# Self-attention cores: probabilities turned four heads at a time, query blocks outermost

## The chip, the core and the metric

The program runs on one NeuronCore of a Trainium2 chip. The engines are TensorE (PE; its weight loads are shown apart as PEld), VectorE (DVE), ScalarE (ACT), GpSimd (POOL) and SyncE (SP), which here only issues DMAs. The metric is the device time of one execution in microseconds, lower is better. The median of three executions of the kernel before is 3642.35 us (3640.83 to 3653.55).

## The reference

A decoder of two layers, each with causal self-attention, cross-attention and a mixture of experts, on x of 2 x 512 tokens of width 512. The change is in the two self-attentions (16 heads of 32). Cut to what matters:

```python
q, k, v = proj(Wq), proj(Wk), proj(Wv)            # B=2, H=16, S=512, dh=32
q, k = _apply_rope(q, cos, sin), _apply_rope(k, cos, sin)   # first layer only
scores = jnp.einsum('bhqd,bhkd->bhqk', q, k) / math.sqrt(dh)
scores = jnp.where(causal, scores, jnp.finfo(jnp.float32).min)
probs = jax.nn.softmax(scores, axis=-1)
attn = jnp.einsum('bhqk,bhkd->bhqd', probs, v)
```

## The kernel before

The stages run one after the other with a barrier between them. `self_attention` (stage names sa0 and sa1; the profile shows both as sa) has four: a layer norm that also turns x (L155, transposes of 128x128), `project_self`, `attention_core` and the output projection (L196). `attention_core` also serves the first cross-attention, where it isn't causal.

Q and K come out of the projection with channels on partitions, four heads of 32 to a chunk of 128, eight chunks (`NI`) for the two sequences. The core splits each value into a high part (L497 on ACT) and the rest (L539 on POOL), and DMAs of 32 rows lay three combinations of the two under each other, so that one product over 96 rows gives nearly exact scores (`packed`, L373 on SP for Q, L550 on POOL for K).

It works on pairs of heads, 16 pairs (`NP`) a core. The scores are made twice. First with queries on the output's partitions (L425, and L427 adds the mask), two heads and one block of 128 queries at a time, for the row maxima (L575 on DVE). The maxima are turned (L438), split into two rows (L503, L584) and laid under `packed` by DMA (L380). Then the scores are made again with keys on partitions, less the maximum (L449 over 98 rows, mask L452). Their exponentials (L511 on ACT) need no turning: they are the moving operand of P times V (L461), whose stationary operand is V beside a block of ones, 64 columns for a head, so that the row sums come out as well. Two heads take columns 0 to 63 and 64 to 127. The result is copied (L517), laid out by four DMAs a pair (L391, L392), and DVE inverts the sums over 128x512 (L590) and multiplies (L592).

Each product of two f32 operands shows as two MATMUL records; a transpose and a product of packed operands (fp32r) show as one.

The order on each engine is written out: TensorE goes through pair j's four key blocks, and behind each comes the P times V of the block before and one query block of pair j+2's maxima. TensorE may start a pair's second scores once `put_rows` has landed, and the maxima of a query block once the block before is reduced.

## Time and profile before

| | |
|---|---|
| median of three executions | 3642.35 us |
| the profiled execution | 3634.11 us, its span 3632.3 us |
| core of sa0, from its barrier to the first product of the output projection | about 123 to 365 us |
| core of sa1 | about 1377 to 1605 us |
| busy over the span | PE 3145.2, DVE 1263.3, ACT 967.4, POOL 975.8 us |
| mean granted TensorE clock | 0.879 |

The profile has one row for each group of instructions with its count and mean, and a trace with the start of each. A granted clock of 0.50 is 1.2 GHz, of 1.00 is 2.4 GHz. A PE record's length holds the way through the array, so what an instruction costs in a stream is the distance from its start to the next one's.

### The profile page before, as it was taken

How to read it: one execution, taken by the hardware profiler on the slowest of the kernel's cores; microseconds unless marked ns; L12 is line 12 of the kernel's file. 1: busy time of each engine (PE TensorE's matmuls, PEld its weight loads, DVE VectorE, ACT ScalarE, POOL GpSimd, SP SyncE). 2: the span in 40 equal slices, each digit the busy share in tenths (PEclk: the TensorE clock that was granted, in tenths of full speed). 3: DMA queues.
4: the chain of work that ended last, by engine and by line, in shares of the span. 5: the costliest groups of instructions: out<-in, count | busy, mean ns of one | idle time of the engine just before them, and what ended most of it. 6: DMA issues, size and time to landing. Idle time of an engine off the chain costs nothing. (4 is left out here: it accounts for less than half of the span.)

```text
span 3632.3 us, 40681 instructions
## 1 busy us (share of the span) xinstructions
PE 3145.2 (87%) x13166; PEld 1910.4 (53%) x13166; DVE 1263.3 (35%) x1863; ACT 967.4 (27%) x2096; POOL 975.8 (27%) x1107
## 2 busy tenths in 40 slices
PE   7898897988559787988996989999999856999997
PEld 3444343333548543447885874555554442777773
DVE  3234335654411213425434225555552131111114
ACT  1233133444101013314332004444442000222220
POOL 2331003220021203303442105555553014222115
PEclk9656897999679887669998999999999957999998
DMA  2232203331059613314443433222220001999996
GB/s 78 56 75 58 84 12 84 75 70 31 25 202 323 222 58 81 80 27 152 142 144 107 142 105 118 68 68 69 71 72 21 25 18 33 340 346 347 331 325 191
DMA packets 317562, 442.93 MB, mean 122 GB/s; under 512 B 45502, under 2 KB 179622, under 8 KB 317448
## 3 DMA queue, kind: packets, MB, share of 16 engines
q1 hardware_dynamic: 276232, 344.96, 29.9%
q0 software_dynamic: 26240, 69.27, 7.0%
q10 hardware_dynamic: 14976, 27.27, 2.1%
q8 instruction: 61, 1.00, 0.1%
q14 instruction: 53, 0.43, 0.0%
HBM read 308.78 MB, written 75.58 MB: 106 GB/s over the span
## 5 line engine op out<-in xcount | busy, mean ns | idle before, releaser
L1379 PE MATMUL ps<-moe_blocks_xgt,moe_blocks_w 128*128 128x128 f32 (+1 forms) x3072 | 364.3, 277 | 7.2 <-DMA moe_blocks_b1s<-rb_cols 4.7
L511 ACT ACTIVATE normed<-ps 128x512 f32<-128x512 f32 (+3 forms) x512 | 247.6, 516 | 427.9 <-PE ps L452 265.2
L1379 PEld LDWEIGHTS ps<-moe_blocks_xgt,moe_blocks_w 128*128 128x128 f32 (+1 forms) x3072 | 350.7, 184 | 13.1 <-issue 12.8
L2258 POOL TENSOR_TENSOR normed<-normed,xa_core_rinv 128x257 f32<-128x257 f32 (+1 forms) x256 | 266.1, 1062 | 273.0 <-DVE xa_core_rinv L2189 273.0
L1361 PE MATMUL ps<-moe_blocks_w,moe_blocks_ht 128*128 128x512 f32 (+1 forms) x624 | 285.1, 593 | 0.0
L2225 ACT ACTIVATE normed<-ps,xa_core_nmax 128x257 f32<-128x257 f32 (+1 forms) x256 | 173.8, 685 | 323.2 <-DVE xa_core_nmax L2184 322.8
L2135 PE MATMUL ps<-xa_core_k,xa_core_q 128*128 128x512 f32 x512 | 242.6, 597 | 14.8 <-DVE xa_core_k L2174 10.9
L2184 DVE TENSOR_REDUCE xa_core_nmax<-ps 128x1 f32<-128x257 f32 (+1 forms) x256 | 164.4, 683 | 250.2 <-PE ps L2135 250.2
L1450 DVE COPY moe_blocks_y<-ps 128x512 f32<-128x512 f32 x104 | 71.9, 692 | 457.4 <-PE ps L1361 457.4
L2161 PE MATMUL ps<-xa_core_pt,xa_core_v 128*128 128x512 f32 x512 | 225.1, 592 | 0.7 <-DVE xa_core_pt L2197 0.7
L578 DVE TENSOR_REDUCE xa_core_nmax<-ps 128x1 f32<-128x1024 f32 x128 | 155.9, 1224 | 133.6 <-PE ps L432 133.6
L575 DVE TENSOR_REDUCE sa_core_nmax<-ps 128x2 f32<-128x256 f32 (+3 forms) x128 | 105.6, 825 | 251.8 <-PE ps L427 251.7
L2149 PEld LDWEIGHTS ps<-identity,normed 128*128 128x128 f32 x1024 | 118.1, 140 | 104.5 <-issue 67.9
L2149 PE MATMUL ps<-identity,normed 128*128 128x128 f32 x1024 | 146.4, 276 | 22.4 <-ACT xa_core_pt L2235 21.5
L1361 PEld LDWEIGHTS ps<-moe_blocks_w,moe_blocks_ht 128*128 128x128 f32 (+1 forms) x624 | 111.1, 191 | 100.5 <-issue 100.5
L1914 POOL TENSOR_TENSOR normed<-normed 128x512 f32<-128x512 f32 x96 | 126.3, 1317 | 138.3 <-DVE normed L1874 138.3
L425 PE MATMUL ps<-sa_core_packed 96*128 96x128 f32 (+3 forms) x256 | 131.0, 571 | 33.3 <-DMA sa_core_packed<-sa_core_parts 23.7
L2161 PEld LDWEIGHTS ps<-xa_core_pt,xa_core_v 128*128 128x128 f32 x512 | 94.8, 190 | 108.1 <-issue 107.1
L461 PE MATMUL ps<-normed,sa_v 128*64 128x256 f32 (+3 forms) x512 | 149.7, 680 | 0.0
L1327 POOL COPY moe_blocks_idx<-moe_index 128x1 uint32 (+1 forms) x104 | 19.2, 185 | 483.1 <-PE ps L1352 438.2
L1400 ACT ACTIVATE moe_blocks_xgt<-ps 128x512 f32<-128x512 f32 x104 | 62.1, 597 | 316.7 <-PE ps L1352 316.7
L461 PE MATMUL ps<-normed,xa_v 128*64 128x512 f32 x512 | 144.1, 643 | 0.0
(292 smaller groups left out, 5447.1 us busy)
## 6 DMA issues: line engine op xcount, KB each, us to landing
moe_blocks_w<-L_ffn_rw SPq DMA_DIRECT2D x80, 704.0 KB
moe_blocks_w<-L_ffn_rw SPq DMA_DIRECT2D x80, 512.0 KB
moe_blocks_w<-L_ffn_w SPq DMA_DIRECT2D x24, 1408.0 KB
moe_y<-moe_blocks_y ACTq DMA_DIRECT2D x104, 256.0 KB
k_raw<-xa_kq_raw SPq DMA_DIRECT2D x64, 256.0 KB, 2.0
v_rows<-normed SPq DMA_DIRECT2D x64, 256.0 KB
xa_core_k<-k_raw SPq DMA_DIRECT2D x32, 512.0 KB, 4.7
xa_core_v<-v_rows SPq DMA_DIRECT2D x32, 512.0 KB
```

The costliest lines, as they stand in the source:

```text
L425: nc.tensor.matmul(g.ps[:, bank + h, 0:w], packed[0:KR, s, h, 0, n * P:(n + 1) * P], packed[0:KR, s, h, 1, 0:w], start=True, stop=False)
L461: nc.tensor.matmul(g.ps[2 * h * DH:2 * (h + 1) * DH, 6 + j % 2, a:S], v[:, j // (H // 2), kb, j % (H // 2), h:h + 2, :].rearrange("p a d - ...
L511: nc.scalar.activation(probs[:, e % RING, a:S], g.ps[:, 4 + h, a:S], ACT.Exp).then_inc(exp_done, 1)
L578: nc.vector.tensor_reduce(nmax[:, j % 2, n:n + 1], g.ps[:, bank:bank + 2, :].rearrange("p a n -> p (a n)"), X_AXIS, ALU.max, negate=True). ...
L1361: mm = nc.tensor.matmul(g.ps[:, 6 + s % 2, :], ht[0:fn, s % 2, f, :], w2s[s][0:fn, f, :], start=(f == 0), stop=(f == NF - 1))
L1379: mm = nc.tensor.matmul(g.ps[0:fn, 2 + s % 2 + 2 * half, f * P:(f + 1) * P], w1s[s][:, k, half * F + f0:half * F + f0 + fn], xgt[:, s % 2, ...
L2135: mm = nc.tensor.matmul(s_ps(n)[:, c:c + 512], q[:, s, qb * P:(qb + 1) * P], k[:, s, c:c + 512], start=True, stop=True)
L2149: mm = nc.tensor.transpose(g.ps[:, 4 + half, m * P:(m + 1) * P], prob[:, nn % PR, c:c + P], g.ident[:, :])
L2161: mm = nc.tensor.matmul(g.ps[:, 6 + hs, :], v[:, hs, m, :], pt[:, hs, m, :], start=(m == 0), stop=(m == NKT - 1))
L2184: ins = nc.vector.tensor_reduce(nmax[:, n % PR, m:m + 1], s_ps(n)[:, lo:hi], X_AXIS, ALU.max, negate=True)
L2225: ins = nc.scalar.activation(prob[:, n % PR, lo:hi], s_ps(n)[:, lo:hi], ACT.Exp, bias=nmax[:, n % PR, m:m + 1], accum_out=rsum[:, n % PR, ...
L2258: ins = nc.gpsimd.tensor_tensor(prob[:, n % PR, lo:hi], prob[:, n % PR, lo:hi], rinv[:, n % PR, m:m + 1].to_broadcast([P, hi - lo]), ALU.mult)
```

## The change

`attention_core` stays for the first cross-attention. The self-attentions get `self_core`:

- Scores are made once, with queries on partitions. A unit is one pair of heads and one block of 128 queries, with the keys up to that block; a chunk of four heads has 8 units (query block outermost, then the two pairs), a core 64.
- DVE reduces the maxima, ACT takes the exponentials with the maximum as bias and the sum accumulated, DVE inverts two numbers a row, POOL multiplies the probabilities by them, TensorE turns them in 128x128 blocks, and DVE (3 of 4 heads) and ACT (1 of 4) copy them to SBUF.
- P times V takes V (32 columns a head) as the stationary operand. Four heads write partitions 0, 32, 64 and 96 of one bank, for one query block of a chunk, one key block after the other.
- Gone are the second scores, the turning, splitting and laying of the maxima, the ones beside V, the layout DMAs and the inversion over 128x512. ACT copies a chunk's result straight to its place.
- The splitting of the first two chunks into parts, and the DMAs that pack them, move into the projection stage. Of later chunks they run in the core, the rest now on DVE, all DMAs on SP (12 a chunk, each with Q and K together).

```diff
+    def low(self, nc, dve, i):
+        dve.wait_ge(self.high_done, i + 1)
+        nc.vector.tensor_tensor(self.parts[i % 2][:, 1:4:2, :], self.qk[:, :, i, :], self.parts[i % 2][:, 0:3:2, :],
+                                ALU.subtract).then_inc(self.low_done, 1)
...
+                if t in (1, 2):
+                    if rope:
+                        act.wait_ge(rotated, len(units))
+                    else:
+                        act.wait_ge(copied, len(units))
+                    heads.high(nc, t - 1)
...
+    NI, QB, U = B * KC, S // P, 2 * (S // P)
+    N = NI * U
+    SKEW, LAG, PR = 3, 2, 6
+    SCORE, TURN, VALUE = (0, 2), (4, 5, 6), 7
...
+                if u >= 2:
+                    pe.wait_ge(exp_done, 2 * (u - 1))
+                t = heads.packed[i % 2]
+                for h in range(2):
+                    nc.tensor.matmul(g.ps[:, bank + h, 0:n], t[:, 2 * p + h, 0, qb * P:n], t[:, 2 * p + h, 1, 0:n],
+                                     start=True, stop=False)
...
+                    for j in range(qb + 1):
+                        mm = nc.tensor.transpose(g.ps[:, bank, j * P:(j + 1) * P],
+                                                 prob[:, 2 * (u % PR) + h, j * P:(j + 1) * P], g.ident[:, :])
...
+                for j in range(qb + 1):
+                    for h in range(HPC):
+                        mm = nc.tensor.matmul(g.ps[h * DH:(h + 1) * DH, VALUE, qb * P:(qb + 1) * P],
+                                              v[:, b, j, c * P + h * DH:c * P + (h + 1) * DH],
+                                              pt[:, at + h, j * P:(j + 1) * P], start=(j == 0), stop=(j == qb))
+                mm.then_inc(pv_done, 1)
...
+            for u in range(N + SKEW):
+                if u < N:
+                    score(u)
+                if u >= SKEW:
+                    turn(u - SKEW)
+                    if u - SKEW >= LAG + 1 and (u - SKEW) % 2 == 1:
+                        i, qb, p, n = place(u - SKEW - LAG)
+                        values(i, qb)
```

TensorE before, in the middle of sa0's core: one key block of a pair, the P times V of the block before it, and one query block of the maxima. L425 and L427 are the maxima's scores, L449 and L452 the second ones, L461 is P times V.

```order
L425 MATMUL ps<-sa_core_packed 128x512
L427 MATMUL ps<-sa_core_mask,identity 128x128
L425 MATMUL ps<-sa_core_packed 128x512
L427 MATMUL ps<-sa_core_mask,identity 128x128
L449 MATMUL ps<-sa_core_packed 128x512
L452 MATMUL ps<-identity,sa_core_mask 128x128
L449 MATMUL ps<-sa_core_packed 128x512
L452 MATMUL ps<-identity,sa_core_mask 128x128
L438 MATMUL ps<-identity,sa_core_nmax 8x128
L461 MATMUL ps<-normed,sa_v 64x128 x2
```

TensorE of the change, at the same place: L390 and L393 are a unit's scores and mask, L412 the transposes of the unit three before (`SKEW`), L429 is P times V of one query block of four heads.

```order
L390 MATMUL ps<-sa_packed 128x256 x2
L393 MATMUL ps<-sa_core_mask,identity 128x128 x2
L412 MATMUL ps<-identity,sa_w 128x128 x8
L429 MATMUL ps<-normed,sa_v 32x128 x12
L390 MATMUL ps<-sa_packed 128x256 x2
L393 MATMUL ps<-sa_core_mask,identity 128x128 x2
L412 MATMUL ps<-identity,sa_w 128x128 x2
L390 MATMUL ps<-sa_packed 128x384 x2
L393 MATMUL ps<-sa_core_mask,identity 128x128 x2
L412 MATMUL ps<-identity,sa_w 128x128 x2
L429 MATMUL ps<-normed,sa_v 32x128 x16
```

The second scores are gone, transposes stand in their place, and P times V comes once in two units, in up to 16 short products instead of two long ones for each key block.

DVE of the change, in the first chunk of a core: L453 is a unit's maxima, L457 the inverted sums of the unit before, L466 and L468 the copies of turned probabilities (two heads, one head), L227 the rest for the chunk after next.

```order
L453 TENSOR_REDUCE sa_core_nmax<-ps 128x2
L457 RECIPROCAL sa_core_rinv<-sa_core_rsum 128x2
L466 COPY normed<-ps 128x2x128
L453 TENSOR_REDUCE sa_core_nmax<-ps 128x2
L457 RECIPROCAL sa_core_rinv<-sa_core_rsum 128x2
L468 COPY normed<-ps 128x128
L227 TENSOR_TENSOR sa_parts<-sa_qk,sa_parts 128x2x512
L453 TENSOR_REDUCE sa_core_nmax<-ps 128x2
L457 RECIPROCAL sa_core_rinv<-sa_core_rsum 128x2
L466 COPY normed<-ps 128x2x256
```

Before, DVE had only the maxima, the small L584 and once in two pairs L590 with L592 between them; now it stands in the path of every unit three times.

## Rows read from the trace of the kernel before

**Rows 1.** Busy time and clock by stretch: both cores, slow and fast stretches, others
```profile
core 0: us, PE busy (x) PEld busy (x) DVE busy (x) ACT busy (x) POOL busy (x), PEclk, DMA share, GB/s
123.00:365.00 242.00, 210.70 (x784) 108.70 (x784) 89.23 (x98) 75.13 (x177) 69.09 (x113) 0.57 0.30 71
1377.00:1605.00 228.00, 194.02 (x784) 100.71 (x784) 89.42 (x98) 74.38 (x177) 68.97 (x113) 0.63 0.32 75
1490.00:1590.00 100.00, 100.00 (x342) 50.15 (x342) 37.98 (x40) 32.26 (x77) 18.97 (x33) 0.50 0.25 59
1406.00:1430.00 24.00, 21.96 (x135) 11.99 (x131) 9.85 (x13) 11.21 (x29) 11.69 (x18) 1.00 0.37 87
2400.00:2700.00 300.00, 288.53 (x1050) 152.68 (x1049) 168.51 (x296) 134.84 (x344) 156.52 (x148) 1.00 0.21 70
1286.00:1290.00 4.00, 4.00 (x21) 4.00 (x20) 2.73 (x6) 2.40 (x4) 0.00 (x0) 0.50 0.79 291
1290.00:1291.50 1.50, 1.48 (x13) 1.25 (x11) 0.00 (x0) 1.34 (x3) 0.00 (x0) 0.97 0.00 0
```

**Rows 2.** The same view of L461 alone; a pair has 16 of its records
```profile
1406.00:1430.00 24.00, 8.16 (x44) 1.98 (x40) 1.00 0.37 87
1490.00:1590.00 100.00, 38.10 (x116) 8.61 (x116) 0.50 0.25 59
```

**Rows 3.** Timeline of PE at 1.2 GHz: start us, length us, then the instruction
```profile
201.72 0.46 PE L449 MATMUL ps<-sa_core_packed 98*128 98x128 f32 x1
...
202.07 0.46 PE L449 MATMUL ps<-sa_core_packed 98*128 98x128 f32 x1
...
202.59 1.12 PE L461 MATMUL ps<-normed,sa_v 128*64 128x256 f32 x4
203.64 0.79 PE L425 MATMUL ps<-sa_core_packed 96*128 96x512 f32 x1
...
204.32 0.77 PE L425 MATMUL ps<-sa_core_packed 96*128 96x512 f32 x1
...
206.85 0.70 PE L461 MATMUL ps<-normed,sa_v 128*64 128x128 f32 x4
207.48 0.47 PE L425 MATMUL ps<-sa_core_packed 96*128 96x128 f32 x1
```

**Rows 4.** Timeline of PE at 2.4 GHz, the same core
```profile
214.46 0.65 PE L461 MATMUL ps<-normed,sa_v 128*64 128x256 f32 x4
215.04 0.50 PE L425 MATMUL ps<-sa_core_packed 96*128 96x512 f32 x1
...
215.43 0.47 PE L425 MATMUL ps<-sa_core_packed 96*128 96x512 f32 x1
...
217.50 0.44 PE L461 MATMUL ps<-normed,sa_v 128*64 128x128 f32 x4
217.87 0.33 PE L425 MATMUL ps<-sa_core_packed 96*128 96x128 f32 x1
...
218.07 0.30 PE L425 MATMUL ps<-sa_core_packed 96*128 96x128 f32 x1
```

**Rows 5.** Timeline of PE in the second cross-attention: transposes of probabilities at 2.4 GHz
```profile
2401.03 1.04 PE L2149 MATMUL ps<-identity,normed 128*128 128x128 f32 x8
```

**Rows 6.** Groups by shape, 2400 to 2700 us: count | busy us, mean ns | idle before
```profile
L2161 PE MATMUL ps<-xa_core_pt,xa_core_v 128*128 128x512 f32 x259 | 114.0, 592 | 0.0
L2258 POOL TENSOR_TENSOR normed<-normed,xa_core_rinv 128x767 f32<-128x767 f32 x66 | 100.0, 1515 | 0.0
...
L2197 DVE COPY xa_core_pt<-ps 128x512 f32<-128x512 f32 x65 | 43.5, 669 | 0.0
L2258 POOL TENSOR_TENSOR normed<-normed,xa_core_rinv 128x257 f32<-128x257 f32 x66 | 40.5, 613 | 142.9 <-DVE xa_core_rinv L2189 142.9
...
L2225 ACT ACTIVATION_READ_ACCUMULATOR normed<-ps,xa_core_nmax 128x1 f32 x131 | 25.7, 196 | 0.0
```

**Rows 7.** The page's costliest groups: maxima of the self-attention cores
```profile
L575 DVE TENSOR_REDUCE sa_core_nmax<-ps 128x2 f32<-128x256 f32 (+3 forms) x128 | 105.6, 825 | 251.8 <-PE ps L427 251.7
```

**Rows 8.** Groups by shape, 156 to 286 us: DVE, ACT
```profile
L511 ACT ACTIVATE normed<-ps 128x512 f32<-128x512 f32 x18 | 10.7, 598 | 25.8 <-PE ps L452 25.2
```

**Rows 9.** Timeline: first product of sa0's core, last values, first product of the projection behind
```profile
134.40 0.45 PE L425 MATMUL ps<-sa_core_packed 96*128 96x128 f32 x1 [12.19 <-DMA sa_core_packed<-sa_core_parts]
...
363.41 0.69 DVE L592 TENSOR_TENSOR sa_qt<-sa_qt,sa_core_total 128x512 f32<-128x512 f32 x1
...
365.32 2.90 PE L196 MATMUL ps<-sa_wo,sa_qt 128*128 128x512 f32 x3 [9.95 <-PEq L67]
```

More of the change, by code:

```diff
@@ L172, in self_attention @@
         w_loaded = [st.sem(f"w_loaded{n}") for n in range(3)]
+        heads = HeadPacks(st, qk)
         def load_weights(sp):
@@ L181, in self_attention @@
         with Stage(nc, name + "_proj") as pr:
-            project_self(nc, g, pr, w, w_loaded, rope, qt, kt, v, wos, wo, wo_loaded, masks, mask)
+            project_self(nc, g, pr, w, w_loaded, rope, qk, v, wos, wo, wo_loaded, masks, mask, heads)
         with Stage(nc, name + "_core") as co:
-            attention_core(nc, g, co, qt, kt, v, ot, S // P, masks)
+            self_core(nc, g, co, heads, v, ot, masks, w)
         with Stage(nc, name + "_out") as ou:
@@ L205, in _, with __init__, high, pack @@
                                                 ALU.add).then_inc(added, 1)
-def project_self(nc, g, st, w, w_loaded, rope, qt, kt, v, wos, wo, wo_loaded, masks, mask):
+class HeadPacks:
+    TERMS = ((0, 0), (1, 0), (0, 1))
+    ROWS = len(TERMS) * DH
+    DMAS = HPC * len(TERMS)
+    def __init__(self, st, qk):
+        self.qk = qk
+        self.parts = [st.sbuf(f"parts{n}", [P, 4, S], F32R) for n in range(2)]
+        self.packed = [st.sbuf(f"packed{n}", [self.ROWS, HPC, 2, S], F32R) for n in range(2)]
+        self.high_done, self.low_done = st.sem("high_done"), st.sem("low_done")
+        self.packed_in = [st.sem(f"packed_in{n}") for n in range(2)]
+    def high(self, nc, i):
+        nc.scalar.activation(self.parts[i % 2][:, 0:3:2, :], self.qk[:, :, i, :], ACT.Copy).then_inc(self.high_done, 1)
+    def low(self, nc, dve, i):
+        dve.wait_ge(self.high_done, i + 1)
+        nc.vector.tensor_tensor(self.parts[i % 2][:, 1:4:2, :], self.qk[:, :, i, :], self.parts[i % 2][:, 0:3:2, :],
+                                ALU.subtract).then_inc(self.low_done, 1)
+    def pack(self, sp, i):
+        sp.wait_ge(self.low_done, i + 1)
+        for h in range(HPC):
+            for r, (qp, kp) in enumerate(self.TERMS):
+                sp.dma_start(self.packed[i % 2][r * DH:(r + 1) * DH, h, :, :].bitcast(F32),
+                             self.parts[i % 2][h * DH:(h + 1) * DH, qp:3 + kp:2 + kp - qp, :].bitcast(F32)
+                             ).then_inc(self.packed_in[i % 2], 16)
+    def wait_packed(self, eng, i):
+        eng.wait_ge(self.packed_in[i % 2], 16 * self.DMAS * (i // 2 + 1))
+def project_self(nc, g, st, w, w_loaded, rope, qk, v, wos, wo, wo_loaded, masks, mask, heads):
     made, copied = st.sem("made"), st.sem("copied")
     v_made, v_copied = st.sem("v_made"), st.sem("v_copied")
-    units = [(c, b, dst, part) for part, dst in enumerate((qt, kt)) for c in range(KC) for b in range(B)]
+    units = [(c, b, qk[:, part, :, :], part) for part in range(2) for c in range(KC) for b in range(B)]
     RAW = 3
@@ L228, in _ @@
             sp.dma_start(masks[:, :], mask).then_inc(wo_loaded, 16)
+            heads.pack(sp, 0)
+            heads.pack(sp, 1)
             sp.wait_ge(wo_loaded, 32)
@@ L276, in _ @@
                 act.wait_ge(v_made, t + 1)
[L277 to L284 removed]
+                nc.scalar.activation(v[:, b, kb, :], g.ps[:, 6 + t % 2, :], ACT.Copy).then_inc(v_copied, 1)
+                if t in (1, 2):
[4 more added lines that the diff above has]
+                    heads.high(nc, t - 1)
+        if rope:
+            @block.gpsimd
+            def _(pool):
                 pool.wait_ge(r_loaded, 48)
@@ L291, in _ @@
                                             ALU.mult).then_inc(cos_done, 1)
[L293 to L304 removed]
+        @block.vector
@@ new lines, in _ @@
+        def _(dve):
+            for j, (c, b, dst, part) in enumerate(units if rope else ()):
+                if j == 0:
+                    dve.wait_ge(r_loaded, 48)
+                dve.wait_ge(swapped, j + 1)
+                nc.vector.tensor_tensor(rs[:, j % 2, :], g.ps[:, 4 + j % 2, :], sin[:, :],
+                                        ALU.mult).then_inc(sin_done, 1)
+                dve.wait_ge(sin_done, j + 1)
+                dve.wait_ge(cos_done, j + 1)
+                nc.vector.tensor_tensor(dst[:, b * KC + c, :], rc[:, j % 2, :], rs[:, j % 2, :],
+                                        ALU.add).then_inc(rotated, 1)
+            heads.low(nc, dve, 0)
+            heads.low(nc, dve, 1)
```

154 lines of the change are left out of this document (130 added, 24 removed).

## The prediction

> **What bounds the kernel now.** First the two stages. The self-attention cores take 242 and 228 us of the span [rows 1], together 470; nothing else in the program is edited but the projections ahead of them. Then who works there. In 1490 to 1590 us TensorE is busy for all of 100.00 us, DVE for 37.98, ACT for 32.26, POOL for 18.97 [rows 1]. So TensorE is the bound. Then its clock: the mean granted clock of the cores is 0.57 and 0.63, and it is 0.50 (1.2 GHz) for the whole of 1490 to 1590, while it is 1.00 in 1406 to 1430 [rows 1]. Then the pace. A pair of heads has 16 records of P times V: 116 in 100 us is 13.8 us a pair at 1.2 GHz, 44 in 24 us is 8.7 us a pair at 2.4 GHz [rows 2]. I count in chunks of four heads: 27.6 us slow, 17.5 us fast, eight chunks a core.
>
> **Does that follow from the parts?** Score products of two heads with their mask: at 128 keys 2 x 0.35 = 0.70 us and at 512 keys 2 x 0.68 = 1.36 us slow [rows 3], 0.40 and 0.78 fast (218.07 less 217.87, 215.43 less 215.04) [rows 4]. The four lengths lie evenly, so a set is 4 x the mean of the ends: 4.1 us slow, 2.4 us fast. P times V of two heads: over 128 queries 0.63 us slow, 0.37 fast; over 256, 1.05 and 0.58 [rows 3, 4]. So 128 queries more cost 0.42 slow and 0.21 fast, on a start of 0.21 and 0.16; the four key blocks (512 to 128 queries) make 5.0 and 2.7 us. A pair is two sets and one P times V: 13.2 slow against 13.8 measured, 7.5 fast against 8.7. Slow, TensorE's own work explains the pace within 5%. Fast, about 16% is waiting on others.
>
> **What goes.** The second scores: 2 x 4.1 = 8.2 us a chunk slow, 4.8 fast. The turned maxima and their DMAs, L590 and the layout DMAs: they were late only at 2.4 GHz and at the ends of the core.
>
> **What TensorE gets.** Transposes: a unit turns 2 blocks for each key block, a chunk 2 x 2 x (1+2+3+4) = 40. The second cross-attention turns the same f32 blocks fast, eight in 1.04 us with the way through the array, so 0.11 to 0.13 each [rows 5]; slow, a layer norm shows 20 weight loads in 4.00 us, 0.20 to 0.21 each [rows 1]. That is 4.6 us fast, 8.4 slow. P times V: 10 key blocks a chunk, each with four heads of 32 columns over 128 queries, 8 records. What this costs no row shows. L461 shows two column groups at work at once: four records of 512 columns one after the other take 0.43 us each in the second cross-attention (114.0 us is 259 records in 300 us, at 592 ns with their way through) [rows 6], 0.11 for 128 columns, while two heads' four records cost 0.21 for 128 and not 0.43. If four groups go at once, a block costs 0.21 fast and 0.42 slow; if only two at once, with the start paid each time, 0.74 and 1.26. I take 0.40 and 0.60, near the lower end: pairs of groups do overlap, but eight short weight loads have little to hide under. A chunk: 4.0 fast (2.1 to 7.4), 6.0 slow (4.2 to 12.6). TensorE's sum for a chunk is then 4.8 + 4.6 + 4.0 = 13.4 us fast and 8.2 + 8.4 + 6.0 = 22.6 us slow.
>
> On how the columns are shared, the Trainium skill (TensorEngine Tiling (Array Packing), Key Properties) says that changing the tiling mode drains the array. The change alternates between full and 32-column products, but so does the kernel before with 64 columns, and the 0.16 to 0.21 us start in my sum is what such a turn shows; charged for every key block instead of every batch it would give about the 0.40 that I take.
>
> **What the others get, a chunk.** DVE: 16 maxima of one head each, in 8 instructions at a mean of 0.825 us [rows 7] = 6.6; copies of 2 and 1 heads over 128 to 512 keys, by 0.669 us for 512 [rows 6] and about 1.05 ns an element more or less: 3.2 + 1.9; the rest of a split over 1024 elements, about 1.2, where L592 is 0.69 for 512 [rows 9]; eight small inversions 1.2. Sum 14.1. ACT: 16 exponentials, where 512 keys take 0.598 [rows 8], 0.44 in the mean, and half of a 0.196 us accumulator read each [rows 6]: 8.6; a quarter of the copies 1.75, high parts 1.05, result 0.6: 12.0. POOL: 0.613 us for 257 and 1.515 for 767 elements [rows 6], so 1.77 ns an element: 0.6, 1.1, 1.5, 2.0 for a unit's 256 to 1024, 10.3 a chunk. SP: 12 DMAs, which have a whole chunk to land. All are under TensorE's slow 22.6; at 2.4 GHz DVE's 14.1 passes TensorE's 13.4 and becomes the bound.
>
> **What ends last at 2.4 GHz.** DVE and TensorE hand over to each other in each unit: reduction waits for scores, scores for the exponentials of two units before, transposes for POOL and for a free bank, the DVE copy for the transposes. Queued behind the copy's wait is the next reduction, for which ACT waits. P times V comes once in two units in one piece (up to 1.6 us), and there DVE waits. The kernel before lost 16% to its waits at that clock; the same on 14.1 gives 16.4. I take 16.5 us a chunk fast; slow 22.6 and 8% for the same reasons, 24.5.
>
> **Head and tail.** The first score of sa0 starts at 134.40, after 12.19 us of waiting for the packing DMAs [rows 9]; the change packs two chunks under the projection of V, which leaves about 1 us. The two high parts and the two rests there lie beside TensorE's products of V, for whose result ACT only has one copy of 512 elements a tile (0.6 us, [rows 8]) and DVE nothing, so they cost nothing; uncovered they would be 2 x (1.05 + 1.2), some 5 us. At the end the last pair's result is laid and inverted until 364.1 and the projection starts at 365.32, 9.95 us after the last product [rows 9]; a copy and a barrier, 2 us, remain. Filling and draining the new chain (POOL 2.0, transposes, copy, last P times V) I put at 8 us. A core is 11 us + 8 chunks.
>
> **The clock.** This decides more than any count. Before, it stayed at 1.2 GHz through 100 us of a full TensorE, and a core in the same shape as the new one, with the same transposes, POOL multiplication and copies, shows 1.00 over 300 us with PE busy for 288.53 [rows 1]. What went ahead of a rise: in the layer norm nothing but transposes, 0.50 until 1290 and 0.97 behind it [rows 1]. The new core replaces half the short packed products by such transposes, and has no DMA or long inversion that stops TensorE for microseconds once it is fast. So I expect 2.4 GHz most of the time, with some 10 us a core lost to slow stretches (two chunks at 24.5 for 16.5 are 16, one is 8).
>
> The Trainium skill (TensorE: Matmul & The Clock Gate, Part 4: PE-mode transpose) says otherwise: a transpose does not count as a busy PE and does not bring the full clock. By it the change would stay slow, which is my first rival. This trace disagrees where it can: the clock rises in a run of f32 transposes alone, from 0.50 to 0.97 [rows 1].
>
> **Forecast.** 11 + 8 x 16.5 = 143, and 10 for slow stretches: 153 us a core, 306 for 470, so 164 less. From the profiled 3634 that is 3470; the median of the runs stands 8 us above it, so 3478.
>
> **Rivals.** 1. The clock stays at 1.2 GHz throughout: 11 + 8 x 24.5 = 207 a core, 56 us less, 3586. For it: 100 us without a rise, and scores of the same kind stay in the mix. 2. The clock changes to and fro, or four column groups don't go at once and a key block costs 0.74 fast: TensorE's 16.8 passes DVE, 19.5 with the handing over; both give a chunk of 19.5 to 20.5, a core of 170 to 180, so 3525 to 3535 (110 to 120 less). 3. Slower than before: the clock stays low and the four heads go two at a time, starting anew each time. A chunk is 8.2 + 8.4 + 12.6 = 29.2 us, a core 245, 20 us more in all: 3662. It decides from 28 us a chunk on, that is from 1.14 us a key block slow; one head at a time (8 x 0.21 and starts) would give 3730. Against it speaks the overlap that L461 already shows. 4. The change doesn't reach its pipelining: DVE's order makes each unit wait for the one before, 20 us a chunk; this falls on the time of rival 2.
>
> **How the numbers follow.** Forecast 0.50, rival 1 0.17, rivals 2 and 4 together 0.24, rival 3 0.05, better than all of them (15 us a chunk and no slow stretch, 3450 and below) 0.04. The range 3440 to 3592 takes in the forecast with a chunk of 15 to 18, rival 2 and rival 1. A measurement of this kernel tells 0.5%, 18 us: faster 0.92, the same 0.04, slower 0.04.
>
> **What would show it.** In the profile of the changed kernel: granted clock near 1.00 in both cores, cores of 150 us; transposes 0.11 us apart; a key block's eight records within 0.40 us; DVE busy 110 us a core and PE's longest waits on DVE or POOL; first scores within 2 us of the barrier, the output projection 2 us behind the last P times V. A clock of 0.50 with PE full is rival 1, and eight records over 0.7 us rival 2. The forecast is wrong if the clock stays low, or if POOL's multiplication over two heads takes much more than 2 us.

## The result and the profile after

| | before | after |
|---|---|---|
| median of the runs, us | 3643.27 (3640.83 to 3653.55, 4 runs) | 3456.27 (3445.77 to 3463.13, 4 runs) |
| ratio to before | 1 | 0.9479 (95% interval 0.9444 to 0.9514) |
| span of the profiled run, us | 3632.3 | 3444.0 |
| mean granted clock of the span | 0.879 | 0.920 |
| core of sa0 / sa1, us | 242 / 228 | 136.9 / 139.5 |

The change takes 187 us off the median and 188 off the span. The two cores lose 470.2 less 276.4 = 194 us, a little more than that, so all of the gain is there. Here and below a core's length runs from DVE's cast of the mask, the first instruction behind the barrier, to the first product of the output projection.

The lines of the changed kernel that the rows name: L390 score products, L393 the mask's product, L412 transposes, L429 P times V, L453 maxima, L457 inversions, L466 and L468 DVE's copies of turned probabilities, L498 ACT's, L487 exponentials, L510 POOL's multiplication, L223 high and L227 rest of a split, L476 the copy of a result, L196 the projection behind.

Busy time and clock by stretch, the view of [rows 1]: both cores; one chunk in the middle; the slow stretch near the start of sa0's core, and the 75 us behind it:

```profile
core 0: us, PE busy (x) PEld busy (x) DVE busy (x) ACT busy (x) POOL busy (x), PEclk, DMA share, GB/s
123.50:260.40 136.90, 112.33 (x1217) 77.56 (x1217) 101.38 (x199) 92.21 (x303) 79.60 (x64) 0.94 0.32 71
1274.50:1414.00 139.50, 115.64 (x1216) 80.24 (x1217) 101.64 (x199) 92.18 (x303) 79.61 (x64) 0.90 0.32 69
163.30:179.60 16.30, 13.24 (x154) 9.10 (x153) 12.84 (x26) 11.53 (x39) 9.94 (x9) 1.00 0.50 110
...
128.00:138.00 10.00, 8.47 (x38) 5.31 (x39) 7.64 (x14) 6.77 (x23) 5.29 (x5) 0.50 0.00 0
...
143.00:218.00 75.00, 60.38 (x705) 41.18 (x705) 59.78 (x117) 52.89 (x173) 44.22 (x38) 1.00 0.45 98
```

The granted clock went from 0.57 and 0.63 [rows 1] to 0.94 and 0.90. TensorE is busy for 82% of sa0's core and DVE for 74%: no engine is full.

Timeline of PE in sa0's core, the view of [rows 3, 4]: start us, length us, instruction, and in brackets the idle time ahead of it and who ended it:

```profile
123.82 0.44 PE L390 MATMUL ps<-sa_packed 96*128 96x128 f32 x2 [1.93 <-DVE sa_core_mask L447]
...
172.82 0.65 PE L429 MATMUL ps<-normed,sa_v 128*32 128x128 f32 x16
173.40 0.44 PE L390 MATMUL ps<-sa_packed 96*128 96x128 f32 x2
...
173.80 1.04 PE L412 MATMUL ps<-identity,sa_w 128*128 128x128 f32 x8
174.60 0.48 PE L390 MATMUL ps<-sa_packed 96*128 96x256 f32 x2
...
176.74 0.86 PE L429 MATMUL ps<-normed,sa_v 128*32 128x128 f32 x24
...
179.60 1.08 PE L429 MATMUL ps<-normed,sa_v 128*32 128x128 f32 x32
...
185.19 0.43 PE L429 MATMUL ps<-normed,sa_v 128*32 128x128 f32 x8 [0.74 <-ACT sa_qk L476]
...
257.01 1.93 PE L429 MATMUL ps<-normed,sa_v 128*32 128x128 f32 x56
260.39 1.96 PE L196 MATMUL ps<-sa_wo,sa_qk 128*128 128x512 f32 x4 [1.45 <-PEq L67]
```

The four query blocks of a chunk have 1 to 4 key blocks of eight records each. They take 0.43, 0.65, 0.86 and 1.08 us with the way through the array. From the start of a batch to the start of the next product it is 0.36, 0.58, 0.79 and 1.01 us (173.40 less 172.82 is 0.58): 0.14 us and 0.22 for each key block. Batches of 32 records start at 146.98, 163.30, 179.60, 195.90 and 212.21 us, so a chunk is 16.3 us. Eight transposes take 1.04 us, as in [rows 5], and 0.80 from start to the next start, 0.10 each.

The waits of the changed kernel, 139 to 250 us: engine and line, who is waited for, us in total, times, longest:

```profile
POOL sa_w L510 <- DVE sa_core_rinv L457: 43.9, 42, 2.1
ACT sa_w L487 <- DVE sa_core_nmax L453: 34.0, 37, 1.7
DVE sa_core_nmax L453 <- PE ps L393: 18.1, 22, 1.8
PEld ps L412 <- DVE normed L466: 14.8, 28, 0.8
...
PEld ps L412 <- ACT normed L498: 8.4, 19, 0.9
PE ps L412 <- DVE normed L466: 7.6, 20, 0.6
...
PE ps L429 <- ACT sa_qk L476: 5.2, 7, 0.7
```

It is a ring: DVE waits for scores, ACT for DVE's maxima, POOL for DVE's inversions, and TensorE for the two copies that free its banks. One more wait, of P times V for ACT's copy of the last chunk's result, comes once a chunk. In the chunk of 16.30 us above, the timeline of DVE shows 3.45 us of idle time: 2.29 waiting for scores, 0.52 for the high part, 0.38 for transposes and 0.26 for an exponential.

Groups by shape, 139 to 258 us, the view of [rows 6] (count, busy us, mean ns, idle before); they are DVE's maxima and copies, the rest of a split, and POOL's longest:

```profile
L510 POOL TENSOR_TENSOR sa_w<-sa_w,sa_core_rinv 128x1024 f32<-128x1024 f32 x16 | 30.0, 1893 | 10.0 <-DVE sa_core_rinv L457 10.0
...
L453 DVE TENSOR_REDUCE sa_core_nmax<-ps 128x2 f32<-128x1024 f32 x14 | 17.0, 1216 | 7.6 <-PE ps L393 7.6
...
L466 DVE COPY normed<-ps 128x1024 f32<-128x1024 f32 x8 | 9.8, 1224 | 3.8 <-PE ps L412 3.8
...
L227 DVE TENSOR_TENSOR sa_parts<-sa_qk,sa_parts 128x1024 fp32r<-128x1024 f32 x5 | 7.5, 1495 | 2.6 <-ACT sa_parts L223 2.6
```

### The profile page after: what moved, and what is told of

Read it like the earlier page. It is cut to its first block and busy times, and to the rows that moved or that the text cites. A ratio compares the mean times of both kernels' runs of the same rounds, so it can differ in the third digit from the quotient of the medians.

```text
span 3444.0 us, 42500 instructions
## 1 busy us (share of the span) xinstructions
PE 2962.6 (86%) x14027; PEld 1856.9 (54%) x14030; DVE 1291.0 (37%) x2069; ACT 1005.3 (29%) x2352; POOL 995.4 (29%) x1007
## 5 line engine op out<-in xcount | busy, mean ns | idle before, releaser
L2342 PE MATMUL ps<-xa_core_k,xa_core_q 128*128 128x512 f32 x512 | 242.3, 597 | 13.4 <-DVE xa_core_k L2381 11.6
L510 POOL TENSOR_TENSOR sa_w<-sa_w,sa_core_rinv 128x256 f32<-128x256 f32 (+3 forms) x128 | 159.2, 1253 | 239.5 <-DVE sa_core_rinv L457 239.5
L718 ACT ACTIVATE normed<-ps 128x512 f32<-128x512 f32 x256 | 138.9, 595 | 160.1 <-PE ps L656 159.9
L487 ACT ACTIVATE sa_w<-ps,sa_core_nmax 128x128 f32<-128x128 f32 (+3 forms) x256 | 132.2, 523 | 81.4 <-DVE sa_core_nmax L453 80.2
L412 PE MATMUL ps<-identity,sa_w 128*128 128x128 f32 x640 | 122.0, 300 | 31.3 <-DVE normed L466 17.1
```

Source lines behind the costliest of these rows:

```text
L510: nc.gpsimd.tensor_tensor(prob[:, 2 * s:2 * s + 2, 0:n], prob[:, 2 * s:2 * s + 2, 0:n], rinv[:, s, :, 0:1].to_broadcast([P, 2, n]), ALU.mu ...
L718: nc.scalar.activation(probs[:, e % RING, a:S], g.ps[:, 4 + h, a:S], ACT.Exp).then_inc(exp_done, 1)
L2342: mm = nc.tensor.matmul(s_ps(n)[:, c:c + 512], q[:, s, qb * P:(qb + 1) * P], k[:, s, c:c + 512], start=True, stop=True)
```

## The experiments

The theory: most of the gain is the clock, brought up by the transposes; four column groups work at once; at 2.4 GHz the chunk is set by the handing over between TensorE and DVE and not by one engine. The experiments tell its parts from their rivals. They ran on chips on which the kernel before took 3624.7 (packing in the core, one group, spare transposes, scores twice), 3647.1 (the change once more, one transpose, POOL splits, filled chunk) and 3624.5 us (head by head, result copied early, short POOL, short maxima), and the ratios given are to that. Between the cores nothing is edited but, in some, the projection of sa1, yet that stretch took from 1003.1 to 1014.7 us in different runs, about as much as some edits cost. So I compare the lengths of the cores first, and times second. A chunk is measured from one batch of 32 records of P times V to the next.

### The change once more

The changed kernel as it is, next to the experiments of the second chip.

> The changed kernel as it is, on the same chip as its variants, so that they can be set against it. Cores of 137 and 140 us as in its profile; if chips differ as the kernel before did (3643 and 3625), the total may be 0.5% lower.

Measured: 3451.39 us, ratio 0.9451 (0.942 to 0.9481), cores 140.0 and 139.6 us at a clock of 0.89 and 0.90. With the profile above, a core of the change is 137 to 140 us, 276 to 280 for both. Its chunks show what a slow stretch costs:

```profile
146.66:163.73 17.07, 14.37 (x154) 10.18 (x153) 12.96 (x26) 11.66 (x39) 10.00 (x9) 0.90 0.43 94
180.79:197.11 16.32, 13.24 (x153) 9.09 (x152) 12.85 (x26) 11.55 (x39) 9.96 (x9) 1.00 0.45 98
213.43:231.55 18.12, 15.56 (x153) 10.99 (x152) 12.94 (x26) 11.56 (x39) 10.00 (x9) 0.81 0.40 88
```

At a clock of 1.00 a chunk is again 16.3 us; at a mean of 0.90 it is 17.1 and at 0.81 it is 18.1. Added up over the chunks behind the first, the four cores of the change seen here lose 0.9, 3.6, 3.3 and 3.6 us to this, and that is nearly all by which 136.9 us differs from 139.5, 140.0 and 139.6. So chunks of two kernels are compared at a clock of 1.00.

### Does the clock, and not the smaller work, carry the gain?

The kernel before, with five spare transposes ahead of each set of score products, 320 a core. Nothing is taken away.

```
                 if causal:
                     w = (n + 1) * P
+                    for m in range(5):
+                        nc.tensor.transpose(g.ps[:, bank, m % 4 * P:(m % 4 + 1) * P], g.x[:, m, 0:P], g.ident[:, :])
```

> The kernel before with work added: ahead of each query block's maxima in the self-attention cores, five transposes of 128x128 f32 (data of the residual) into the bank that the scores then overwrite, 20 a pair of heads, 40 a chunk, as many as the change has. Theory: transposes bring TensorE to 2.4 GHz, as in the layer norm. Then a pair takes 7.5 + 20 x 0.11 = 9.7 us of TensorE and with waits 11 to 11.5 for 13.8: the cores get shorter although they do more, 60 to 90 us less than before, 3555 to 3585, granted clock near 1.00 there. Rival (transposes don't count as a busy TensorE; the low clock has another cause): the clock stays at 0.50, a pair takes 13.2 + 20 x 0.21 = 17.4 us, 32 pairs 115 to 135 us more, 3760 to 3780.

Measured: 3563.24 us, ratio 0.9846 (0.9795 to 0.9897). Busy time and clock by stretch, of both cores and of the 100 us from 200 on:

```profile
123.50:330.10 206.60, 164.00 (x1104) 106.39 (x1104) 89.24 (x98) 71.41 (x177) 69.13 (x113) 0.93 0.35 83
1342.50:1547.80 205.30, 163.94 (x1104) 106.31 (x1105) 89.22 (x98) 71.22 (x177) 68.97 (x113) 0.94 0.36 83
200.00:300.00 100.00, 88.41 (x612) 56.88 (x610) 50.00 (x54) 37.90 (x96) 33.56 (x56) 1.00 0.38 88
```

Its cores have 1104 products for 784 [rows 1], and are 35 and 23 us shorter: the clock went from 0.57 and 0.63 to 0.93 and 0.94, and in the 100 us in the middle it is 1.00 with TensorE busy for 88, where the kernel before had 0.58 and 97 from 200 to 300 us, and 0.50 and 100 in its other core [rows 1]. Five transposes take 0.52 us from their start to the next product's, so 320 are 33 us of work, and the cores are shorter all the same: the higher clock gives back 68 and 56 us, 1.7 to 2 times what the transposes cost. The rival, by which transposes leave the clock low and only add their work, is refuted. Whether added work of another kind would have raised the clock as well, no run here tests.

The other way round: the changed kernel with only the first block of each head's probabilities turned, 16 transposes a chunk for 40 (the other blocks are left out).

```
-                    for j in range(qb + 1):
+                    for j in range(1):
                         mm = nc.tensor.transpose(g.ps[:, bank, j * P:(j + 1) * P],
```

> The changed kernel with only the first 128x128 block of each head's probabilities turned (16 transposes a chunk for 40; the rest of the turned probabilities is stale, which is what is left out). The copies stay whole. Theory: the transposes are what brings the clock up; with 40% of them the clock is at 0.50 for much longer than in the change (mean of the cores 0.6 to 0.8 instead of 0.92), and the time is the same or longer in spite of 2.6 us of TensorE less a chunk: +0 to +40 us. Rival: the clock stays at 1.00 as in the change and DVE with the handing over sets the pace: a chunk 15.5 to 16.3 us, 0 to 12 us less.

Measured: 3470.65 us, ratio 0.9497, and 19 us slower than the change on the same chip. Its cores:

```profile
123.30:270.30 147.00, 114.04 (x1025) 76.72 (x1025) 102.61 (x199) 92.22 (x303) 79.86 (x64) 0.69 0.30 66
1284.10:1428.20 144.10, 112.26 (x1024) 75.14 (x1024) 102.39 (x199) 92.21 (x303) 80.94 (x64) 0.69 0.30 67
```

192 of 1217 products fewer, the other engines as before, and the granted clock falls from 0.90 to 0.69. The cores are 7 and 4.5 us longer; most of the other 8 us lie in the stretch between them, which nothing edits. So in the changed kernel too the clock falls when transposes go. Other work can hold it up there as well: with the scores made twice it is 0.97 (below), and with P times V in one group 0.96.

On this the Trainium skill (TensorE: Matmul & The Clock Gate, Part 4: PE-mode transpose) says that a transpose doesn't count as busy and doesn't bring the full clock. Both runs disagree: with f32 transposes added the clock rose from 0.57 to 0.93, and with them taken away it fell from 0.90 to 0.69.

### Does the slow start of the core matter?

The change runs at 0.50 from 128 to 138 us. This kernel puts eight spare transposes ahead of each unit's scores in the first chunk.

```
+                for m in range(8 if u < U else 0):
+                    nc.tensor.transpose(g.ps[:, bank, m % 4 * P:(m % 4 + 1) * P], g.x[:, m, 0:P], g.ident[:, :])
                 t = heads.packed[i % 2]
```

> The changed kernel with eight spare transposes ahead of each unit's scores in the first chunk of each core, into the bank that the scores then overwrite (64 a core, 0.9 us a unit at 2.4 GHz). In the change the clock is at 0.50 from 5 us after a core's start to about 16 us. Theory: the transposes keep TensorE at 2.4 GHz there, the first chunk's other work then runs faster, and the time is within 8 us of the change either way, with a granted clock of 1.00 in the first 16 us. Rival: they only add 8 x 0.9 to 1.7 us to the first chunk, 7 to 14 us a core, and the clock still falls.

Measured: 3451.44 us, ratio 0.9458, beside 3451.39 for the change; cores 140.2 and 138.9 us beside 140.0 and 139.6. The clock is 0.96 and 0.98 for 0.89 and 0.90 (1.00 from 128 to 138 us), and the time is the same. The first batch of 32 records starts 25.93 and 24.63 us into the core, for 24.16 and 23.41: the 64 transposes, 6.4 us of work, cost 1.2 to 1.8 us of time beyond what the clock gave. The chunks behind lose 1.7 us a core to slow stretches, for 3.3 and 3.6. So the two nearly cancel. How long the first chunk would take at full clock without the spare work, no run shows; behind it slow stretches cost at most 3.6 us a core, and not the 10 that I had set aside.

### Are four column groups at work at once, and what decides it?

First, all four heads' P times V into the same 32 columns, one head after the other (the results of three heads are lost).

```
-                for j in range(qb + 1):
-                    for h in range(HPC):
-                        mm = nc.tensor.matmul(g.ps[h * DH:(h + 1) * DH, VALUE, qb * P:(qb + 1) * P],
+                for h in range(HPC):
+                    for j in range(qb + 1):
+                        mm = nc.tensor.matmul(g.ps[0:DH, VALUE, qb * P:(qb + 1) * P],
```

> The changed kernel with P times V of the four heads one after the other, all into the same 32 columns (so three heads of four are lost: what is left out is their results, not their work). Theory: side by side, a key block of four heads costs 0.22 us at 2.4 GHz, one after the other 8 records x 0.107 = 0.86, so TensorE gets 10 x 0.64 = 6.4 us a chunk more, 18.6 in all, passes DVE, and a chunk takes 19.5 to 21 us for 16.3: 50 to 75 us more, 3505 to 3530, clock as in the change. Rival: the records of one head overlap too, or DVE stays the bound, then under 15 us more. If the clock falls with it, over 100 us more.

Measured: 3517.74 us, ratio 0.9718; cores 183.1 and 183.0 us at a clock of 0.96. Timeline of PE:

```profile
173.34 3.68 PE L429 MATMUL ps<-normed,sa_v 128*32 128x128 f32 x32
...
180.59 1.03 PE L429 MATMUL ps<-normed,sa_v 128*32 128x128 f32 x8 [0.74 <-ACT sa_qk L476]
```

3.68 less 1.03 for three more key blocks is 0.88 us each for 0.22, four times as much: in the changed kernel all four groups work at once. A chunk is 21.8 us (173.34 to 195.16), 5.5 more than the change's. Both cores together are 87 to 90 us longer, more than the 50 to 75 expected; the time lies in the expected range only because this chip is faster (3624.7 for 3643.3 us with the kernel before).

This edit moved the heads' columns and the order. The next one keeps the columns of the change and swaps the loops alone.

```
-                for j in range(qb + 1):
-                    for h in range(HPC):
+                for h in range(HPC):
+                    for j in range(qb + 1):
```

> The changed kernel with the two inner loops of P times V swapped: all key blocks of one head, then the next head, so up to eight records in a row go to the same 32 columns before the next 32 are used. Work and places are the same. Theory (records of different column groups overlap only if they stand next to each other in the order): a batch costs nearly what it did with all heads in one group, 0.88 us a key block and not 0.22, the chunk is 21 to 22 us, the time 3495 to 3525. Rival (TensorE starts whatever group is free, or waits for the group alone): 0.22 us a key block as in the changed kernel, and its time within 6 us.

Measured: 3449.53 us, ratio 0.9516 (0.9471 to 0.9561), on the chip where the kernel before took 3624.5; cores 150.2 and 148.5 us, some 10 longer than the change's. Timeline of PE:

```profile
179.35 1.59 PE L429 MATMUL ps<-normed,sa_v 128*32 128x128 f32 x24
...
182.94 2.46 PE L429 MATMUL ps<-normed,sa_v 128*32 128x128 f32 x32
...
188.97 0.43 PE L429 MATMUL ps<-normed,sa_v 128*32 128x128 f32 x8 [0.75 <-ACT sa_qk L476]
...
192.91 0.66 PE L429 MATMUL ps<-normed,sa_v 128*32 128x128 f32 x16
```

Neither side was right. With two or four records in a row to the same columns (8 and 16 in the batch) the groups overlap as before, 0.43 and 0.66 us; with six in a row 1.59 us stand for 0.86, and with eight 2.46 for 1.08. So the order of the records decides from somewhere between four and six in a row on. A chunk grows by the 2.1 us of the two long batches on TensorE and by 1.2 us in length (17.5).

The Trainium skill (TensorE: Matmul & The Clock Gate, Part 3: Packing small matmuls — row/col tiling) says that products stay in program order at start and end, and measures 2.38 times the speed for three column tiles of 32 columns (512 moving columns). A dependence on the order agrees with it; the factor here is 4.0 for four groups of f32 products over 128 columns, by 0.88 and 0.22 us.

### What is the first packing worth?

The first two chunks' split and packing DMAs taken out of the projection of V and put at the start of the core (the same calls of `high`, `low` and `pack`, moved).

```
-            heads.pack(sp, 0)
-            heads.pack(sp, 1)
...
-            for i in range(2, NI):
-                sp.wait_ge(scores, U * (i - 1))
+            for i in range(NI):
+                if i >= 2:
+                    sp.wait_ge(scores, U * (i - 1))
                 heads.pack(sp, i)
```

> The changed kernel with one part undone: the splitting and packing of the first two chunks stand at the start of the core again instead of under the projection of V. Theory: this part alone is worth the wait for the packing DMAs, some 9 to 10 us a core, so about 3475 us against 3456 of the change, and the first score product starts 10 us behind the barrier. Rival: the wait was hidden by something else that is late anyway (the core's slow first chunk), then it costs under 4 us a core, up to 3464. If TensorE's idle time ahead of the first product also lowers the clock for longer, it costs more than 12 us a core.

Measured: 3455.22 us, ratio 0.9544 (0.9497 to 0.9591). Its cores:

```profile
123.60:274.00 150.40, 114.57 (x1217) 79.74 (x1217) 103.89 (x201) 94.23 (x305) 79.61 (x64) 0.89 0.39 85
1285.70:1434.80 149.10, 113.00 (x1216) 78.12 (x1217) 103.94 (x201) 94.22 (x305) 79.57 (x64) 0.90 0.39 86
```

They are 9.5 to 13.5 us longer than the change's, and the ratio is 0.0065 to 0.0093 higher, 24 to 34 us of the whole. The first score product starts 12.5 us behind the cast (136.06), for 0.3 in the change; [rows 9] had shown 12.19 us of waiting. The expected 3475 us stood for a kernel before of 3643; by the ratio it came out so. The overlap with V's projection is real and free: sa0's core starts at the same place behind it in the change and here (123.5 and 123.6 us).

### What sets the 16.3 us of a chunk?

TensorE is busy for 13.24 us of a chunk, DVE for 12.84, ACT 11.53, POOL 9.94. First more work for TensorE: score products and mask products of each unit twice (the second overwrites the first).

```
+                for again in range(2):
+                    for h in range(2):
+                        nc.tensor.matmul(g.ps[:, bank + h, 0:n], t[:, 2 * p + h, 0, qb * P:n], t[:, 2 * p + h, 1, 0:n],
+                                         start=True, stop=False)
+                    for h in range(2):
+                        mm = nc.tensor.matmul(g.ps[:, bank + h, qb * P:n], g.ident16[:, :], mask16[:, :], start=False,
+                                              stop=True)
```

> The changed kernel with each unit's score products and masks made twice into the same banks, so that TensorE has the same packed products as the kernel before. Theory A: the short packed products with masks are what held the clock low; with twice as many the clock falls to 0.50 for long stretches and a chunk takes 27 to 30 us, 150 us or more above the change, 3610 and up. Theory B: with the transposes in the mix the clock stays at 1.00; TensorE's fast sum of a chunk is 12.2 + 4.8 = 17 us, a chunk 18.5 to 20, 35 to 60 us more than the change, 3490 to 3515.

Measured: 3450.24 us, ratio 0.9525; cores:

```profile
122.50:272.60 150.10, 135.00 (x1472) 99.66 (x1472) 103.20 (x199) 92.55 (x303) 79.59 (x64) 0.97 0.30 65
1276.20:1426.40 150.20, 134.96 (x1473) 99.71 (x1473) 103.28 (x199) 92.57 (x303) 79.56 (x64) 0.97 0.30 65
184.57:202.56 17.99, 16.33 (x185) 12.00 (x185) 13.20 (x26) 11.56 (x39) 9.95 (x9) 1.00 0.41 89
```

From start to next start the second set takes 0.38, 0.44, 0.56 and 0.67 us for a unit of 128 to 512 keys: 4.1 us more TensorE work a chunk, and not the 4.8 of the expectation. It cost 10 to 13 us a core and, at full clock, 1.7 us a chunk (17.99 for 16.30): two fifths. The rest went into the time that TensorE had waited, at a clock that stayed up. Of the clock theory B was right; its 35 to 60 us in all were too many, the two cores are 21 to 24 us longer. TensorE is not the bound alone.

Then less work for POOL: it divides only the first 128 keys of each block (the other probabilities stay undivided).

```
-                nc.gpsimd.tensor_tensor(prob[:, 2 * s:2 * s + 2, 0:n], prob[:, 2 * s:2 * s + 2, 0:n],
+                nc.gpsimd.tensor_tensor(prob[:, 2 * s:2 * s + 2, 0:P], prob[:, 2 * s:2 * s + 2, 0:P],
...
```

> The changed kernel in which POOL divides only the first 128 keys of each query block by the sum (the other probabilities stay undivided, so this part of the computation is left out). POOL's 10.3 us a chunk become 5 (eight instructions of about 0.6 us). Theory A (the way of a unit through DVE, ACT and POOL to the transposes sets the chunk): the chunk falls from 16.3 to 14 to 15 us, 20 to 35 us less in all. Theory B (DVE's own work and its order set it, POOL is only in the shadow): the chunk falls by at most 0.5 us, 0 to 8 us in all.

Measured: 3424.70 us, ratio 0.9445 (0.94 to 0.949), cores 136.6 and 135.0 us, together 5 to 8 less than the change's. One chunk of it at full clock:

```profile
196.52:212.57 16.05, 13.04 (x154) 9.07 (x153) 12.59 (x26) 11.54 (x39) 4.90 (x9) 1.00 0.45 100
```

POOL's 9.94 us are 4.90 and the chunk is 0.25 us shorter, a twentieth of it: theory B. POOL runs in the shadow of the others.

Then less work for DVE: the maxima over the first 128 keys only. Any shift gives the same probabilities as long as the exponentials don't overflow.

```
-                    nc.vector.tensor_reduce(nmax[:, u % PR, :], g.ps[:, bank:bank + 2, 0:n], X_AXIS, ALU.max,
+                    nc.vector.tensor_reduce(nmax[:, u % PR, :], g.ps[:, bank:bank + 2, 0:P], X_AXIS, ALU.max,
...
```

> The changed kernel in which DVE takes the maxima over the first 128 keys only (any shift gives the same probabilities). DVE loses 3072 elements of some 1.05 ns a chunk, 3.2 us, and ACT's wait for each maximum gets shorter. Theory B (DVE's work and order set the chunk): the chunk falls by 2 to 3 us to 13.5 to 14.5, 30 to 50 us less in all. Theory A (the way through POOL sets it): under 1 us a chunk, 0 to 15 us. A kernel in which another part of DVE's work was moved had gained nothing; if this gains nothing either, neither engine alone is the bound.

Measured: 3408.24 us, ratio 0.9399 (0.9353 to 0.9444), the fastest of all. Both cores and one chunk:

```profile
123.60:248.90 125.30, 105.48 (x1216) 74.85 (x1216) 77.47 (x199) 91.89 (x303) 79.26 (x64) 0.96 0.35 77
1263.60:1389.00 125.40, 105.55 (x1217) 74.92 (x1217) 77.65 (x199) 91.94 (x303) 79.23 (x64) 0.96 0.35 77
174.73:189.83 15.10, 12.74 (x154) 9.02 (x153) 9.85 (x26) 11.55 (x39) 9.90 (x9) 1.00 0.46 99
```

3.0 us less DVE work a chunk (9.85 for 12.84) gave 1.2 us of chunk and, with the filling at the start and fewer slow stretches, 12 to 15 us a core. That is more than theory A allowed, and the chunk falls by about half of what B asked: DVE's work is in the bound, and is not the whole of it. Added TensorE work shows to two fifths (1.7 of 4.1), removed DVE work to two fifths (1.2 of 3.0); neither engine alone sets the chunk. That it is the ring through which each unit goes (TensorE's scores, DVE's maxima, ACT's exponentials, and the copies that free TensorE's banks) is read from the waits. For ACT no run changes the work of a unit, so its share is not shown, nor which link is late next once DVE is short.

### Two attempts to shorten the ring by moving work

ACT's copy of a chunk's result one unit earlier, since TensorE waits 0.74 us a chunk for it.

```
-                if u % U == SKEW + LAG and u >= U and u < N:
+                if u % U == SKEW + LAG - 1 and u >= U and u < N:
```

> The changed kernel with ACT's copy of a chunk's result moved one unit ahead, right behind the last P times V that it copies. In the changed kernel TensorE waits for that copy 0.74 us a chunk before the next P times V. If the chunk is a sum of such waits: 0.5 to 0.74 us a chunk, 8 to 12 us in all. Rival (the loop between the engines sets the chunk and the wait moves elsewhere): within 5 us of the changed kernel.

Measured: 3423.37 us, ratio 0.9448 (0.9403 to 0.9493); cores 137.7 and 136.3 us. Both together are 2 to 6 us shorter than the change's. One chunk at full clock:

```profile
162.90:179.05 16.15, 12.95 (x153) 9.03 (x152) 12.84 (x26) 11.66 (x39) 9.99 (x9) 1.00 0.45 99
```

0.15 us of the 0.74 is gained. The wait for the copy is gone, but from 139 to 250 us the waits for ACT's copies of turned probabilities (L498) are 13.7 us on the weight loads and 9.1 on the products, where they were 8.4 and 3.4. The wait moved. The ratios of 0.9448 and 0.9451 or 0.9479 are too close to show a gain of this size.

Then the same, and the rest of each split (L227) on POOL, at the first unit of the chunk, in place of DVE at its fifth.

```
-                if u < N and u % U == 4 and u // U + 2 < NI:
-                    heads.low(nc, dve, u // U + 2)
...
+                if u % U == 0 and 1 <= u // U < NI - 1:
+                    heads.low_pool(nc, pool, u // U + 1)
```

> The changed kernel with two edits at the pace of a fast chunk (16.3 us). The rest of the splitting (1.2 to 2.1 us a chunk) goes from DVE to POOL, at the first unit of the next chunk, and ACT's copy of a chunk's result stands one unit earlier, so that the next chunk's P times V doesn't wait for it (0.74 us in the change). Theory: DVE and its handing over to TensorE set the pace, so a chunk gets 1.5 to 2.2 us shorter, cores 12 to 17 us shorter, 20 to 30 us in all. Rival: TensorE waits for POOL's multiplication (busy 1.9 us of each 2 us unit at 512 keys), and POOL's 2.5 us more delays it: no gain or up to 10 us loss.

Measured: 3453.47 us, ratio 0.9454, beside 3451.39 for the change; cores 141.3 and 138.6 us. DVE's busy time fell from 101.7 to 93.5 us a core, and nothing was gained. The waits of this kernel, 145 to 250 us (its score products are L395), POOL, the DMA queue and PE in its timeline, and the same DMAs and product in the change's:

```profile
PEld ps L395 <- DMA sa_packed<-sa_parts: 6.3, 6, 1.9
...
PE ps L395 <- DMA sa_packed<-sa_parts: 4.8, 6, 1.7
```

```profile
176.75 2.35 POOL L232 TENSOR_TENSOR sa_parts<-sa_qk,sa_parts 128x1024 fp32r<-128x1024 f32 x1
...
179.20 8.81 SPq L239 DMA_DIRECT2D sa_packed<-sa_parts  x12
...
189.85 0.44 PE L395 MATMUL ps<-sa_packed 96*128 96x128 f32 x2 [0.53 <-DMA sa_packed<-sa_parts]
```

```profile
170.13 7.72 SPq L234 DMA_DIRECT2D sa_packed<-sa_parts  x12
...
187.19 0.42 PE L390 MATMUL ps<-sa_packed 96*128 96x128 f32 x2
```

The rest of a split ends at 179.1, and only then do the packing DMAs of the next chunk begin, 10.65 us ahead of its first score product at 189.85, which waits for them. In the change they begin 17.06 us ahead and have landed 9 us before the product. This kernel therefore does not show what 1.5 us less on DVE is worth, since it put a new wait in its place; the one with short maxima does. My expectation of 20 to 30 us looked at the engine that got lighter and not at the transfer queued behind the moved step.

## Why the prediction came out as it did

The forecast was 3478 us, in a range of 3440 to 3592, and 3456 was measured: the mechanism was in the main the forecast's own, and not one of the rivals. By its steps:

- **The clock: right.** 0.94 and 0.90 in the cores, with no rival 1 (3586) in sight. That the transposes cause it, which rested on one layer norm [rows 1], was shown from both sides: cores of 0.93 and 0.94 with them added to the kernel before, 0.69 with three fifths of them gone. That only they would do it was not shown. How much of the gain is the clock is an estimate: a fast chunk of the kernel before is 17.5 us, so eight of them and some 22 us of head and tail [rows 9] would be 162 us a core, 73 under the mean of 235; the step from there to 138 is 24. So about three quarters of the gain is the clock.
- **TensorE's sum for a chunk: too high, at no cost to the forecast.** 13.4 us were predicted and 13.24 are busy, but these are two things: busy time also holds the way through the array each time that TensorE stops. From start to next start, as the prediction counted, a chunk of the change has 4.3 us of scores (0.40, 0.47, 0.57 and 0.69 for a unit), 4.0 of transposes (eight in 0.80) and 2.7 of P times V (0.36 + 0.58 + 0.79 + 1.01): 11.0 for 4.8 + 4.6 + 4.0. The largest miss is P times V: I took 0.40 us a key block, and measured are 0.22 and 0.14 a batch. The lower end of my own range (0.21, four groups at once) was the truth. I had argued that eight short weight loads have little to hide under; nothing of them shows while neighbours in the order go to different columns. The error did no harm because TensorE's sum alone does not set the chunk.
- **DVE, ACT and POOL: right.** 14.1, 12.0 and 10.3 were counted, 12.84, 11.53 and 9.94 us are busy. The single durations fit (1.216 us for the maxima of 1024, 1.224 for the copy, 1.893 on POOL for the 2.0 counted); the sum of DVE is under mine because the records of neighbours overlap by almost 0.1 us each. One was longer: the rest of a split is 1.495 us in the mean, for 1.2.
- **The chunk: right in size, loose in its reason.** 16.5 were predicted and 16.3 measured. "DVE is the bound" is too simple: 3.0 us off DVE give 1.2, 4.1 us on TensorE cost 1.7. That DVE and TensorE hand over to each other, as the prediction said, is what the waits show. The size of it, 16% carried over from the waits of TensorE in a kernel of another shape, had no such ground; that it fits is partly luck.
- **Head and tail: right.** The first scores start 0.3 us after the cast; the packing in the projection is worth 9.5 to 13.5 us a core; the projection behind starts 1.45 us after the last product ends, for the 2 us counted.
- **Filling and slow stretches: mis-sized, and this is the miss.** A core was 11 + 8 x 16.5 + 10 = 153 us. Measured are 136.9 and 139.5, which is 8 x 16.3 + 6.5 and + 9.1. So filling, draining and slow clock cost 6.5 to 9 us together, where I had 21. Two cores make 26 us of the 30 by which the cores are shorter than forecast (194 for 164). Behind the first chunk slow stretches cost 0.9 to 3.6 us a core and not 10; the rest of them lies in the first chunk, where the ring fills and TensorE waits anyway. I had counted both in full, one after the other.
- **The rivals.** Nothing of rival 1 or 3. Rival 2's clock changing to and fro is there in single chunks (17.1 and 18.1 us at 0.90 and 0.81), and not as a state of the core. Its price for groups not at once was 19.5 to 20.5 us a chunk; forced into one group, the chunk is 21.8. Rival 4, DVE's order making each unit wait, is there only as the idle fifth of TensorE. Two sums at the edges were loose: a chunk of 15 us without slow stretches gives 131 us a core and 3434, not 3450, and the 3730 for one head at a time leaves out the starts that it names.

## What to carry to other kernels

Ask of a stage whose engine is full at the lower clock whether more work of another kind would bring the clock up: here, 320 transposes added to each core, with nothing removed, made it 23 to 35 us shorter, and fewer of them made the changed kernel's cores 4.5 to 7 us longer. Do not add a slow stretch and a filling pipeline in a sum when both lie in the same microseconds. When work moves to an idle engine, follow what is queued behind it, DMAs first; and when several engines hand over to each other at 80% each, an edit need not show in full: here two fifths of the work added or taken away on TensorE and DVE, and a twentieth on POOL, at 60%.

## What the runs showed that I had not expected

- Four groups of 32 columns work wholly at once in f32, 0.22 us a key block for 0.88, and each batch has a start of 0.14 us. Whether they do depends on the order of the records: up to four in a row to the same columns cost nothing (0.66 us for 16), eight in a row cost more than twice (2.46 for 1.08).
- The clock rose with transposes added to the kernel before and fell when the changed kernel had fewer of them, though TensorE then had less to do. A chunk with a slow stretch in it is 0.8 to 1.8 us longer, also in a kernel whose mean clock is 0.90.
- DVE's subtraction over 1024 elements is 1.495 us in the mean and POOL's 2.35.
- The stretch between the two cores took 1003.1 to 1014.7 us from run to run, and the unchanged kernel 3624 and 3647 us on different chips. Differences of ten microseconds in the whole time are read from the stage itself.
